# Who issues the 21 early "late pieces" of a graph network's last stretch: SyncE or ScalarE

## What is computed

```python
msg_in = concatenate([x[src], edge_attr])          # 400000 x 192
h = relu(msg_in @ W1.T + b1)
agg = segment_sum(h @ W2.T + b2, dst)              # 12500 x 128
r, z, n = gates(agg @ Wih.T + bih, x @ Whh.T + bhh)
x = layernorm(x + (1 - z) * n + z * x)
mean = segment_sum(x[dst], src) / max(degree, 1)   # second layer, rows by src
x = layernorm(x + mean @ weight + x @ root_weight + bias)
```

## Time and profile before

| | us |
|---|---|
| runs, not profiled | 4222.50, 4222.97, 4232.51 |
| median | 4222.97 |
| profiled execution | 4234.13 |
| its span, first to last instruction | 4232.7 |
| TensorE matmul busy | 3850.8 (91%) |
| ScalarE busy | 2350.7 (56%) |
| GpSimd busy | 3047.4 (72%) |
| VectorE busy | 2821.0 (67%) |

### The profile page before, as it was taken

How to read it: one execution, slowest core, us unless ns; L and a number is a source line. 1 busy time by engine, 2 the same in 40 slices (tenths; PEclk the granted TensorE clock), 3 DMA queues, 4 the chain that set the end, 5 groups by cost and what they waited for, 6 DMA issues and landing times.

```text
span 4232.7 us, 87235 instructions
## 1 busy us (share of the span) xinstructions
PE 3850.8 (91%) x30236; PEld 3421.7 (81%) x30236; DVE 2821.0 (67%) x7211; ACT 2350.7 (56%) x4230; POOL 3047.4 (72%) x3223
## 2 busy tenths in 40 slices
PE   5688999998999998999999999999998999999986
PEld 4667888797979787978888888879797979787875
DVE  4676667666666666666666666766666666666547
ACT  2476555556555555555555556555655555555414
POOL 2677777777777777777777777777777777777731
PEclk8798999999999898999999999999999999899999
DMA  7744657575757565666666565757575756566556
GB/s 204 147 142 133 174 148 181 147 182 141 187 142 183 146 177 149 173 159 166 162 162 167 154 174 147 182 144 183 144 185 143 184 145 178 149 172 156 156 138 158
DMA packets 1016895, 683.91 MB, mean 162 GB/s; under 512 B 818071, under 2 KB 857316, under 8 KB 1016073
## 3 DMA queue, kind: packets, MB, share of 16 engines
q1 hardware_dynamic: 828003, 292.94, 29.6%
q0 software_dynamic: 104320, 217.85, 19.5%
q10 hardware_dynamic: 84134, 167.43, 12.4%
HBM read 497.94 MB, written 179.87 MB: 160 GB/s over the span
## 4 chain that ended last, share of the span: by engine, by line
PE 32%; POOL 31%; issue 13%; DVE 8%; DMA 7%; ACT 3%; DVEq 0%; SPq 0%; POOLq 0%; ACTq 0%
POOL ring L903 25%; PE stream_psw L1397 9%; PE stream_pse L1374 7%; PE stream_pse L1382 7%; PE stream_psa L1391 6%; POOL stream_yg L903 6%; DMA ring<-y,ring 5%; DVE stream_col L1109 2%; ACT stream_a_sb L1002 2%; DMA stream_yg<-y,ring 1%; ACT stream_hid L933 1%; DVE ring L1087 1%; DVE stream_row L1104 1%; PE stream_psw L1434 1%; DVE stream_twin L1092 1%
## 5 line engine op out<-in xcount | busy, mean ns | idle before, releaser
L903 POOL DMA_INDIRECT ring<-y,ring x2495 | 2376.8, 953 | 768.5 <-issue 711.3
L1002 ACT CAST stream_a_sb<-stream_psa 98x512 fp8e3<-98x512 f32 x3125 | 1756.4, 586 | 1128.3 <-PE stream_psa L1391 1070.5
L1391 PE MATMUL stream_psa<-stream_col,stream_row 128*98 128x256 f16 x6250 | 1174.3, 288 | 194.2 <-ACT stream_a_sb L1002 148.0
L1397 PE MATMUL stream_psw<-stream_strip,stream_z 128*128 128x256 fp8e3 x9130 | 1297.1, 274 | 21.6 <-DVE stream_sums L1119 18.1
L1087 DVE TENSOR_TENSOR ring<-stream_pse,ring 128x384 f32<-128x384 f32 x1000 | 486.1, 486 | 967.6 <-DMA ring<-y,ring 810.0
L1382 PE MATMUL stream_pse<-w1b,ring 128*128 128x128 f32 x6250 | 1028.8, 299 | 62.5 <-DVE ring L1087 38.3
L1109 DVE TENSOR_TENSOR stream_col<-stream_psa,stream_twin 128x1536 f16<-128x1536 f16 x1250 | 1016.6, 815 | 0.0
L1391 PEld LDWEIGHTS stream_psa<-stream_col,stream_row 128*98 128x98 f16 x6250 | 734.8, 131 | 323.8 <-ACT stream_a_sb L1002 227.7
L1397 PEld LDWEIGHTS stream_psw<-stream_strip,stream_z 128*128 128x128 f16 x9130 | 891.0, 98 | 123.2 <-issue 31.7
L1382 PEld LDWEIGHTS stream_pse<-w1b,ring 128*128 128x128 f32 x6250 | 873.2, 206 | 108.9 <-issue 66.1
L1374 PEld LDWEIGHTS stream_pse<-stream_seg,stream_hid 128*128 128x128 f32 x6250 | 794.2, 202 | 1.4 <-ACT stream_hid L933 0.8
(11 more groups left out here) (205 smaller groups left out, 1594.9 us busy)
## 6 DMA issues: line engine op xcount, KB each, us to landing
A<-stream_a_sb ACTq DMA_DIRECT2D x625, 245.0 KB
stream_strip<-A SPq DMA_DIRECT2D x1862, 80.0 KB
ring<-in_ea_blocks_dram SPq DMA_DIRECT2D x625, 160.0 KB
ring<-y,ring POOLq DMA_INDIRECT x2500
stream_yg<-y,ring POOLq DMA_INDIRECT x625
prologue_xt<-in_xT_dram SPq DMA_DIRECT2D x14, 448.0 KB, 5.8
y<-prologue_ysb SPq DMA_DIRECT2D x14, 448.0 KB, 4.5
out_dram<-stream_hid ACTq DMA_DIRECT2D x24, 256.0 KB, 3.7
```

What stands on the lines that cost most here:

```text
L903: nc.gpsimd.indirect_dma_start(out=yg[s.c % YR][:, t, :], out_offset=None, in_=h.y, in_offset=bass.IndirectOffsetOnAxis(ap=idx[s.c // (PH ...
L1002: nc.scalar.copy(a_sb[n % AR][0:RW, j, :], psa[BANK[j]][0:RW, :], saturate=False).then_inc(a_out, 1)
L1391: last = nc.tensor.matmul(psa[BANK[j]][0:RW, e * LOS:(e + 1) * LOS], row1[s.c % 2][:, 2 * j + e, :], col1[s.c % 2][:, 2 * j + e, :], start ...
L1397: last = nc.tensor.matmul(bank[:, 0:LOS], zz[:, n // 2, n % 2, :], tiles[:, n // 2, :], start=(first and n == 0), stop=(final and n == hi ...
```

## The change

ScalarE issues the 21 pieces, three behind the relu and the gate work of each of blocks 5 to 11, and in block 5 waits first for the stores of A. SyncE no longer issues them; it still issues the 28 pieces behind the stream and all strips. LATE_RING stays at 21.

```diff
-LATE_FROM, LATE_EACH = 6, 3
-LATE_RING = LATE_EACH * (TAIL - LATE_FROM)
+LATE_FROM, LATE_EACH = 5, 3
+LATE_RING = LATE_EACH * (TAIL - 1 - LATE_FROM)
...
+        def load_strip(eng, ph, c, to, arrived):
+            n, at = ph.tiles * (P // 2), ph.n(PN // 2)
+            for e in range(2):
+                eng.dma_start(to[e::2, 0:ph.tiles, :].bitcast(fp16),
+                             h.A[at // AG][e * C + c:e * C + c + 1, at % AG * LH:(at % AG + n) * LH].rearrange("a (t g l) -> (a g) t l", g=64, l=LH)
+                             ).then_inc(arrived, 16)
...
-                if k is not None and ph.p == ITER:
-                    if k == LATE_FROM:
-                        for x in range(AR):
-                            sp.wait_ge(a_stored[x], 16 * uses(x, BLOCKS))
-                    if k >= LATE_FROM:
-                        for c in range(LATE_EACH * (k - LATE_FROM), LATE_EACH * (k - LATE_FROM + 1)):
-                            load_late(c)
-                    if k == 9:
-                        store_r(ph)
+                if k == 9 and ph.p == ITER:
+                    store_r(ph)
...
             def load_late(c):
-                if c >= LATE_RING:
-                    sp.wait_ge(strip_done, ITER * C + EARLY + c - LATE_RING + 1)
-                load_strip(LAST[1], c, late[c % LATE_RING], late_in_of(c))
+                sp.wait_ge(strip_done, ITER * C + EARLY + c - LATE_RING + 1)
+                load_strip(sp, LAST[1], c, late[c % LATE_RING], late_in_of(c))
...
                 if k is not None:
                     gate_work(k, ph)
+                if not counted(s.c) and LATE_FROM <= k < TAIL - 1:
+                    if k == LATE_FROM:
+                        for x in range(AR):
+                            act.wait_ge(a_stored[x], 16 * uses(x, BLOCKS))
+                    for c in range(LATE_EACH * (k - LATE_FROM), LATE_EACH * (k - LATE_FROM + 1)):
+                        load_strip(act, LAST[1], c, late[c % LATE_RING], late_in_of(c))
```

More of the change, by code:

```diff
@@ L821, in load_phase @@
                 sp.dma_start(deg2[0:1, 0:n], h.deg[:, bass.ds(ph.n(PN), n)]).then_inc(deg_in, 16)
[L823 to L828, removed]
             def store_r(ph):
@@ L855, in body @@
                             reach(sp, strip_done, ph.n(C))
-                        load_strip(ph, c, strip[c % RING], strip_in[c % RING])
+                        load_strip(sp, ph, c, strip[c % RING], strip_in[c % RING])
                 if k is not None and ph.p and k == (3 if ph.p < ITER else 5):
                     store_r(Phase(0, ph.p - 1))
-                if k is not None and ph.p == ITER:
-                    if k == LATE_FROM:
-                        for x in range(AR):
-                            sp.wait_ge(a_stored[x], 16 * uses(x, BLOCKS))
-                    if k >= LATE_FROM:
-                        for c in range(LATE_EACH * (k - LATE_FROM), LATE_EACH * (k - LATE_FROM + 1)):
-                            load_late(c)
-                    if k == 9:
-                        store_r(ph)
+                if k == 9 and ph.p == ITER:
+                    store_r(ph)
             def load_late(c):
-                if c >= LATE_RING:
-                    sp.wait_ge(strip_done, ITER * C + EARLY + c - LATE_RING + 1)
-                load_strip(LAST[1], c, late[c % LATE_RING], late_in_of(c))
+                sp.wait_ge(strip_done, ITER * C + EARLY + c - LATE_RING + 1)
+                load_strip(sp, LAST[1], c, late[c % LATE_RING], late_in_of(c))
             sp.sem_inc(r_stored, 1)
@@ L881, in load_last @@
                 sp.wait_ge(strip_done, ITER * C + (before if before <= EARLY else EARLY + before))
-                load_strip(LAST[0], c, strip[c % RING], strip_in[c % RING])
+                load_strip(sp, LAST[0], c, strip[c % RING], strip_in[c % RING])
             for c in range(STREAMED, EARLY + RING):
```

## The result

The changed kernel took 4215.03 us, the median of 20 runs (4210.22 to 4225.57); the kernel before, 4224.44 us in 20 runs beside it (4219.35 to 4233.76). The ratio is 0.9975, 95% interval 0.9968 to 0.9982: about 10.6 us faster, between 7.6 and 13.5. In a later comparison the same kernel gave 0.998 (0.9971 to 0.999). The forecast was 4215.1 us and a gain of 7.89 us.

A forecast was written before the change was run, and what follows sets the result against it. Late edge attributes behind SyncE's queue were taken to bound blocks 9 to 12. Gain 5.16 + 0.64 + 0.33 + 1.76 = 7.89 us, so 4222.97 - 7.89 = 4215.1 us; range 4208 to 4227.

The forecast's parts named there:

- The reading of the waits: Blocks 9 to 12: TensorE idles 5.16 us for edge attributes queued late on SyncE; all four waits would end.
- ScalarE's price and room: ScalarE, blocks 5 to 11: 0.65 us an issue, 3.9 us for six, hidden behind other work and costed at nothing.
- sign of being wrong: ScalarE's queue: late-piece issues above 0.8 us would show the forecast wrong.
- One sign: TensorE's blocks 8 to 12 would stay within 5.5 to 6.0 us if the forecast was right.
- The page's rule: DMA queues: a second issuing engine saves only issuing time; by that alone no gain, 4223 us; chance 0.04.
- The clock term: Block 12: at the full clock it takes 5.51, not 7.27 us, gaining 1.76 us; bounds 0 and 1.76.
- restarts: TensorE groups after waits: lost overlap of 0.64 us at four places, longer products of 0.33 us at three.
- The base: Whole kernel: the median of three unprofiled runs before, 4222.97 us, from which the gain of 7.89 us was subtracted.
- That the transfers set the arrival: Attribute loads: land later among simultaneous loads, or the clock falls anyway; 4216.9, 4219 to 4220, or 4223 us; chance 0.17.
- ScalarE as the new bound: ScalarE's queue replaces SyncE's: slower once an issue costs over 0.98 us, 4249 us at 1.60; chance 0.04.
- The spread: Whole kernel: runs 10 us apart exceed the gain; a higher middle run gives a 4224.6 us median; chance 0.20.

The follow-up runs named there:

- The doubled issues: The changed kernel with ScalarE issuing every late piece twice, the second time into unread spare buffers: 4235.73 us, ratio 1.0038 to the kernel before.
- attributes on ScalarE: The kernel before with the edge attributes of blocks 7 to 12 issued by ScalarE, late pieces still on SyncE: ratio 0.9996 to the kernel before.
- SyncE kept busy: The changed kernel with SyncE issuing six more loads a block in blocks 6 to 12, into unread spare buffers: ratio 1.0011 to the kernel before.
- before, filled: The kernel before with unread matmuls ahead of TensorE's attribute waits in blocks 9, 10 and 12: ratio 0.9993 to the kernel before.

## Why the prediction was right

**The queue.** The reading of the waits held. They were the landing of attributes held up by SyncE's order; with the late pieces gone all four vanish, and with the queue refilled they return (4.19 us). Attributes leave 0.03 to 0.10 us after their condition, as forecast.

**ScalarE's price and room.** 0.65 us an issue was taken from SyncE's rows; the trace has 3.91 to 3.93 us for six, and 4.18 to 5.54 in three blocks. The 5.54 us of block 9 are 0.92 us an issue, above the 0.8 that the prediction gave as a sign of being wrong; the other two traces have 5.50 and 5.05 us there, so it is no chance. It cost nothing, since those issues end at 4067.72 and the next relu starts at 4068.29. The sum had no term for it, and what makes it is not shown; SyncE issues strips at the same time. Block 6's relu starts 4.39 us after its block (4.31 before), not 0.6 us late; TensorE never waits for a relu in blocks 5 to 12. One sign missed by a little: block 9 takes 6.31 us (4058.00 to 4064.31), not 5.5 to 6.0. Room ahead of block 12's relu is 1.8 us against the 1.0 expected, since the sum counted the relu and the six issues one after the other, and they run together. The doubled issues show what lies past the limit.

**The page's rule.** An issuing engine is worth only its issuing time, says the Trainium skill ("DMA: Bandwidth & Descriptors", "Issuing engines are not separate DMA queues"). The trace agrees that nothing else is saved, and shows that this was all of it: the transfers are the same, the pieces land no sooner, and the time of issuing was in line ahead of a load that TensorE needed.

**The clock term** is the term that was mis-sized. I put it at 1.76 us, between 0 and 1.76, from one execution. With the idle time inside it taken off, the excess of the stretch over 29.18 us is 2.7, 2.6 and 6.8 us in the three traces of the kernel before (up to 0.97 of it restarts, by the prediction's working). A low clock can last through two blocks, as in the third, and then it costs 5 us in block 10 alone, so 1.76 was no upper end. The execution that I read happened to be the middle one, and that is luck: read from the third, the same sum would have given 10.3 us. The mean of the three is 8.2 us; measured were 10.6 (7.6 to 13.5) and 8.4 (4.2 to 12.2).

**The base.** Taking the difference from the stretch and subtracting it from the median, rather than forecasting from the span, was needed: the span read was some 9 us long for a reason in blocks 0 to 4. That the forecast of 4215.1 us met the measured 4215.03 to a tenth is luck too: the base, 4222.97 from three runs, was 1.5 us below the 4224.44 of twenty, and the forecast gain 1.5 us below the 9.4 between the two medians. What is left between 8.2 and 10.6 us is inside the interval, and no trace shows a second source.

**Rivals.** That the transfers set the arrival: refuted by the kernel with attributes on ScalarE, where all transfers stay and no wait does. ScalarE as the new bound: refuted at this price, confirmed at twice the number of issues. The spread did not decide once 20 runs were taken.

## What to carry to other kernels

Sum what an in-order DMA queue issues in each block, at the measured time per issue, and compare it with the block's length: below it an issue is free, above it every load behind it is late, whoever needs it. Move the issues that fill the queue, not the one load that is late, or the lateness comes out at the next load on that queue. An engine with idle time can take them as long as issues and its own work fit in the block. And a stage with waits on TensorE must be read from several executions, since what came on top of 3.6 to 5.2 us of waits differed by 4 us (2.6 to 6.8).

## What the runs showed of the hardware

Issues of the same load cost ScalarE what they cost SyncE at best (3.9 us for six). The price is not fixed: while SyncE issued strips, six took ScalarE 5.54, 5.50 and 5.05 us in block 9 of the changed kernel's three traces, and yet 4.13 us on SyncE and 4.19 on ScalarE, at the same time, with SyncE kept busy; SyncE, with ScalarE issuing nothing, once took 4.95 (before, filled). Issues overlap the ScalarE instruction ahead of them and hold back the next one until the last is out (0.04 us between last issue and relu with doubled issues), so they count as ScalarE's time though the profile does not count them as busy. The clock falls to 1.2 GHz after a TensorE wait in some executions and not in others: after 1.82 us it stayed at 1.00 in the first trace of the kernel before, after 1.30 us it fell in the second, and after 2.41 us it stayed low for most of 13 us in the third, with TensorE busy for all of the window 4070 to 4075. With matmuls in the waits of blocks 0, 4 and 5 it stayed at 1.00 from block 0 to the end of the stream, in the one trace taken.
